# First loop of an LM tower kernel: masks moved to ScalarE, single factors, and the key and value tables made from two products each

## The reference, cut to what matters

```python
tok = wte[input_ids]                                   # rows of 192
Q = layer_norm(tok, gamma, beta) @ W_proj.T            # 8 heads of 64
V = tok @ W_val.T
Q_store = Q[:, :, :-2, :] * arrow_mask                 # tokens followed by a link id
Q_erase = Q_store / norm(Q_store)
erase = einsum('bhip,bhiq->hpq', Q_erase, einsum('bhip,hpq->bhiq', Q_erase, traces)) / denom
traces = 0.99 * (traces - erase) + 0.1 * einsum('bhip,bhiq->hpq', Q_store, V[:, :, 2:, :]) / denom
h = (Q shifted by one token @ traces) @ W_out.T
x = layernorm(h)
q, k, v = split(x @ W_qkv + b_qkv)                     # scores from q k^T
gw = softmax(gelu(v @ W_gp))
```

## Time and profile before

| what | value |
|---|---|
| median of three runs | 459.62 us |
| the profiled execution's own time | 457.82 us |
| its span on the core | 456.0 us |
| first loop, third to last product of queries | 18.48 to 60.65 us |
| between the loops, `prepare("kA")` to `mixed(0)` | 67.49 to 84.09 us |
| second loop | from 84.09 us on |
| TensorE's granted clock in these stretches | 1.00 |

### The profile page before, as it was taken

The page is one execution under the profiler, slowest core; times in us unless marked ns, Lnnn a source line. Parts: engine busy times, 40 slices in busy tenths (PEclk is TensorE's granted clock), DMA queues, the critical chain, the costliest instruction groups (busy, mean ns, idle before and its releaser), DMA issues.

```text
span 456.0 us, 8360 instructions
## 1 busy us (share of the span) xinstructions
PE 432.1 (95%) x3114; PEld 357.1 (78%) x3114; DVE 297.5 (65%) x779; ACT 228.1 (50%) x415; POOL 141.8 (31%) x235
## 2 busy tenths in 40 slices
PE   7898998998999999989999999999999899999995
PEld 5666666798788887878888888899975587787895
DVE  6799882486766657767777668766875253453564
ACT  5566742598833644744322557888864312122220
POOL 5666700375100007620003491013631331211310
PEclk9999999999999999999999999999999999999999
DMA  2115300200100000500000000004539999999404
GB/s 89 43 46 161 115 2 0 105 1 2 30 0 1 0 1 0 201 9 1 0 0 1 2 0 1 1 1 183 234 130 418 379 354 381 388 367 378 169 19 138
DMA packets 14231, 49.64 MB, mean 109 GB/s; under 512 B 3504, under 2 KB 8528, under 8 KB 9968
## 3 DMA queue, kind: packets, MB, share of 16 engines
q1 hardware_dynamic: 7584, 43.21, 25.3%
q0 software_dynamic: 2912, 3.37, 2.6%
q10 hardware_dynamic: 3696, 2.54, 1.8%
HBM read 45.94 MB, written 3.15 MB: 108 GB/s over the span
## 4 chain that ended last, share of the span: by engine, by line
PE 64%; DVE 13%; DMA 12%; POOL 4%; ACT 3%; issue 3%; SPq 0%; ACTq 0%; POOLq 0%; DVEq 0%
DMA w1r<-in_p_w 11%; PE ps L924 8%; PE ps L970 8%; PE ps L1126 5%; PE ps L1067 3%; PE ps L904 2%; PE ps L1096 2%; PE ps L950 2%; PE ps L951 2%; PE ps L952 2%; PE ps L954 2%; PE ps L953 2%; PE ps L1113 2%; DVE qw L1601 2%; DVE ss L1591 1%
## 5 line engine op out<-in xcount | busy, mean ns | idle before, releaser
L924 PE MATMUL ps<-pr,et 128*128 128x192 f32 x256 | 46.2, 331 | 1.6 <-DVE et L1790 1.2
L1126 PE MATMUL ps<-ys,ct 128*128 128x192 f32 x256 | 45.2, 330 | 0.7 <-DMA ys<-ys_dram 0.7
L1965 DVE TENSOR_TENSOR res<-ps,res 128x384 f32<-128x384 f32 x64 | 35.7, 558 | 14.2 <-PE ps L1126 9.7
L924 PEld LDWEIGHTS ps<-pr,et 128*128 128x128 f32 x256 | 41.2, 189 | 4.5 <-ACT et L1349 2.7
L1126 PEld LDWEIGHTS ps<-ys,ct 128*128 128x128 f32 x256 | 41.2, 190 | 4.1 <-issue 2.7
L590 POOL DMA_DIRECT2D ys<-ys_dram x32 | 19.7, 619 | 69.2 <-DMA ys_dram<-ysb 68.0
L1465 ACT ACTIVATE hs<-ps 128x384 f32<-128x384 f32 x16 | 7.8, 490 | 57.9 <-PE ps L1067 57.9
L506 POOL TENSOR_SCALAR ve<-mv 128x1 f32<-128x1 f32 x32 | 10.1, 314 | 81.7 <-DVE mv L1805 41.4
L1338 ACT ACTIVATE scs<-ps,pr 128x1024 f32<-128x1024 f32 x16 | 17.8, 1114 | 29.9 <-PE ps L872 29.9
L1956 DVE COPY ysb<-ps 128x192 f32<-128x192 f32 x16 | 5.7, 357 | 39.5 <-PE ps L1096 39.5
L1342 ACT ACTIVATE zz<-zz,nmx 128x1024 f32<-128x1024 f32 x16 | 18.4, 1151 | 26.0 <-DVE nmx L1784 25.8
(11 more groups left out here) (315 smaller groups left out, 1189.5 us busy)
## 6 DMA issues: line engine op xcount, KB each, us to landing
w1r<-in_p_w SPq DMA_DIRECT2D x16, 1152.0 KB, 19.4
w2r<-in_p_w SPq DMA_DIRECT2D x16, 1152.0 KB, 19.3
ys_dram<-ysb ACTq DMA_DIRECT2D x16, 96.0 KB, 8.7
ys<-ys_dram POOLq DMA_DIRECT2D x32, 48.0 KB, 7.2
phT<-in_p_phi SPq DMA_DIRECT2D x1, 1024.0 KB, 4.7
wT<-in_p_qkv SPq DMA_DIRECT2D x1, 774.0 KB, 5.8
out<-res SPq DMA_DIRECT2D x3, 192.0 KB, 3.4
out<-res ACTq DMA_DIRECT2D x3, 192.0 KB, 3.8
```

The lines of the kernel that those rows point to most:

```text
L924: last = mm(d[:, 0:D], et[:, k, :], pr[:, b * KT + k, 1:1 + D], start=(k == 0), stop=(k == KT - 1))
L1126: last = mm(bank(5 + q % 3)[:, h * D:(h + 1) * D], ct[:, u % 2, k + h, :], ys[:, t % YR, b, :], start=True, stop=True)
L1965: v.tensor_tensor(res[:, i:i + 2, :], bank(5 + q % 3)[:, 0:2 * D].rearrange("p (h d) -> p h d", h=2), res[:, i:i + 2, :], ALU.add).then_in ...
```

## The change

- `xm` is made for all 16 tiles by ScalarE (`masked` there), at the end of its step.
- The token table is passed with the last 64 columns of each row once more (`p_wte`, rows of 256 instead of 192 elements), `tok` has 256 columns, and `normalise` is one operation over 256 columns.
- `nmean` goes; GpSimd makes `nmr` from mean, `rstd` and -1. All factors are single. VectorE takes statistics two tiles ahead from step 3 on. GpSimd's gathers are re-ordered to this.
- `k`, `n` and `v` have two products each (A and B). For B, ScalarE copies the 66 rows to `B2`, then copies rows 0 to 63 of `B2` to `B1` (from SBUF); VectorE writes the remainder into rows 64 to 127 of `B1`.
- `kA` moves from in front of the update to behind the `n` products, its rounding to step 1 of the second loop; `mixed(3)`, which uses its bank, waits for that. `kB` stands where kB1 stood. The bias products go to bank 7 on their own, with their own copy by VectorE. `vB2` and its place in step 3 go.

```diff
-        tok = sb("tok", [P, NX, D], where=front0)
+        tok = sb("tok", [P, NX, XC], where=front0)
...
-        SETUP = ["beta", "kA", "kB1", "kB2", "nB2", "nB1", "nA", "vA", "vB1", "vB2"]
-        SETUP_BANK = [7, 7, 6, 7, 6, 4, 5, 5, 6, 5]
+        SETUP = ["beta", "kB", "nA", "nB", "kA", "vA", "vB"]
+        SETUP_BANK = [7, 6, 5, 4, 7, 6, 5]
...
-                    tok[:, g, :], None, a["L0_tok_wte"], bass.IndirectOffsetOnAxis(ap=ints[:, g:g + 1], axis=0)
+                    tok[:, g, :], None, a["p_wte"], bass.IndirectOffsetOnAxis(ap=ints[:, g:g + 1], axis=0)
...
+            def front_factors(i):
+
+                pool.wait_ge(m["front_stats"], i + 1)
+                link(nc.gpsimd.tensor_tensor(rstd[:, i:i + 1], ve[:, i:i + 1], mhalf[:, 0:1], ALU.pow))
+                nc.gpsimd.tensor_scalar(nmr[:, i:i + 1], mv[:, i, 0:1], rstd[:, i:i + 1], -1.0,
+                                        ALU.mult, ALU.mult).then_inc(m["front_rstd"], 1)
...
-            pool.wait_ge(m["xm_ready"], MV)
-            for i in range(MV, NT):
-                if i + 5 < NX:
-                    gather(i + 5)
-                masked(i)
-                if i % 2 == 0 and i + 2 < NT:
-                    front_factors(i + 2, i + 4)
+            for i in range(3, NT):
+                if i + 2 < KT:
+                    gather(i + 2)
+                elif i == KT - 2:
+                    gather(KT)
+                    gather(KT + 1)
+                elif i < KT + 2:
+                    gather(i + 3)
+                elif i == KT + 2:
+                    gather(KT + 5)
+                    gather(KT + 6)
+                elif i + 4 < NX:
+                    gather(i + 4)
+                front_factors(i)
...
-            prepare("kA", 1)
-
...
-            prepare("kB1", 0)
+            prepare("kB", 0)
...
-            pe.wait_ge(m["setup_taken"], at["kA"] + 1)
+            pe.wait_ge(m["setup_taken"], at["beta"] + 1)
             for t in range(HP):
-                mm(setup_bank("kB2")[:, 272 + 2 * t:274 + 2 * t], wpT[DB:DB + 1, 1, t * P:(t + 1) * P],
-                   ones[DB:DB + 1, 0:2], start=True, stop=True)
-            prepare("kB2", at["kA"] + 1)
-
-            pe.wait_ge(m["mm_ready"], 2)
-            pe.wait_ge(m["setup_taken"], at["kB2"] + 1)
-            for name, free in (("nB2", at["kB1"] + 1), ("nB1", 0), ("nA", 0)):
+                last = mm(bank(7)[:, 2 * t:2 * t + 2], wpT[DB:DB + 1, 1, t * P:(t + 1) * P], ones[DB:DB + 1, 0:2],
+                          start=True, stop=True)
+            last.then_inc(m["mix_done"], 1)
+
+            pe.wait_ge(m["mm_ready"], 3)
+            for name in ("nA", "nB"):
...
-            pe.wait_ge(m["setup_taken"], at["nA"] + 1)
+            prepare("kA", 0)
+            pe.wait_ge(m["setup_taken"], at["nB"] + 1)
+            pe.wait_ge(m["setup_hi"], hi_at["nB+"] + 1)
...
+                if i == 3:
+                    pe.wait_ge(m["setup_taken"], at["kA"] + 1)
...
-                if s == 3:
-                    prepare("vB2", at["vA"] + 1)
...
-                sc.activation(xh[:, i % 3, 0:D], tok[:, t, :], ACT.Identity, bias=nmr[:, i:i + 1], scale=rstd[:, i:i + 1])
-                sc.activation(xh[:, i % 3, D:D + DB], tok[:, t, P:D], ACT.Identity, bias=nmr[:, i:i + 1],
-                              scale=rstd[:, i:i + 1]).then_inc(m["xh_ready"], 1)
+                sc.activation(xh[:, i % 3, :], tok[:, t, :], ACT.Identity, bias=nmr[:, i:i + 1], scale=rstd[:, i:i + 1]
+                              ).then_inc(m["xh_ready"], 1)
+
+            def masked(i):
+                act.wait_ge(m["xh_ready"], i + 1)
+                sc.activation(xm[:, i, 0:D], xh[:, i % 3, 0:D], ACT.Copy, scale=mask[:, i:i + 1]).then_inc(m["xm_ready"], 1)
...
+                    sc.activation(B2, d[0:DB + 2, 0:n], ACT.Copy, scale=scale[1]).then_inc(m["setup_hi"], 1)
+                    act.wait_ge(m["setup_hi"], hi_at[name] + 1)
+                    sc.copy(B1[0:DB], B2[0:DB].bitcast(F32)).then_inc(m["setup_hi"], 1)
...
+                if 2 <= s <= NT:
+                    masked(s - 2)
+                if s == NT:
+                    masked(NT - 1)
...
-                if s in (1, 2, 4):
-                    round_v({1: "vA", 2: "vB1", 4: "vB2"}[s])
+                if s == 1:
+                    round_k("kA")
+                if s in (2, 3):
+                    round_v({2: "vA", 3: "vB"}[s])
...
+                    v.scalar_tensor_tensor(B1[DB:P], d[0:DB, 0:n], scale[1], f(B2[0:DB]), ALU.mult, ALU.subtract)
                     last = remainder(B2[DB:DB + 1, :], d[DB:DB + 1, 0:n], scale[2], B2[DB:DB + 1, :])
...
-                v.tensor_scalar(nmean[:, i:i + 1], mv[:, i, 0:1], -1.0, None, ALU.mult)
...
-                if s <= KT + 1:
-                    return {KT + 1: [KT + 2, KT + 3]}.get(s, [s + 1] if s >= 2 else [])
+                if s <= 3:
+                    return {2: [3], 3: [4, 5]}.get(s, [])
                 return [s + 2] if s + 2 < NT else []
...
-            for name in SETUP[4:7]:
+            dve.wait_ge(m["mix_done"], 3)
+            v.tensor_copy(wpn[:, :, XC:PC], bank(7)[:, 0:2 * HP].rearrange("p (t c) -> p t c", c=2)).then_inc(m["mm_ready"], 1)
+            for name in ("nA", "nB"):
                 round_n(name)
```

More of the change, by code:

```diff
@@ L44, in build @@
 def build(nc, a, out):
-    D = a["L0_tok_wte"].shape[1]
+    D = out.shape[-1]
     _, _, HD = a["p_wp"].shape
@@ L62, in build @@
     PC = P + 2 * DB + 2
-    CB1, CB2 = P, P + DB
+    CB2 = P + DB
     XC = P + 2 * DB
@@ L175, in build @@
         xm = sb("xm", [P, NT, D + 1], where=front)
-        nmean = sb("nmean", [P, NT], where=front)
         ss = sb("ss", [P, NT, HEADS], where=front)
@@ L364, in pass_tiles @@
             return []
-        SETUP = ["beta", "kA", "kB1", "kB2", "nB2", "nB1", "nA", "vA", "vB1", "vB2"]
-        SETUP_BANK = [7, 7, 6, 7, 6, 4, 5, 5, 6, 5]
+        SETUP = ["beta", "kB", "nA", "nB", "kA", "vA", "vB"]
+        SETUP_BANK = [7, 6, 5, 4, 7, 6, 5]
         at = {n: k for k, n in enumerate(SETUP)}
-        PARTS = {"A": (0, P), "B1": (CB1, P), "B2": (CB2, DB + 2)}
+        PARTS = {"A": (0, P), "B": (CB2, DB + 2)}
+        HI = [n + part for n in SETUP for part in (("", "+") if n[1] == "B" else ("",))]
+        hi_at = {n: k for k, n in enumerate(HI)}
         def setup_bank(name):
@@ L480, in _ @@
             for g in range(3):
                 gather(g)
-            front_factors(0, 1)
-            front_factors(1, 2)
+            for i in range(2):
+                front_factors(i)
             gather(3)
-            front_factors(2, 3)
+            front_factors(2)
             gather(4)
[L487 to L493, removed]
@@ L1250, in _ @@
             last.then_inc(m["update_taken"], 1)
-            round_k("kB1")
+            round_k("kB")
             act.wait_ge(m["mix_done"], 1)
@@ L1255, in _ @@
             last.then_inc(m["mm_ready"], 1)
-            round_k("kB2")
-            for name in SETUP[4:7]:
+            for name in ("nA", "nB"):
                 round_n(name)
@@ L1521, in round_off @@
             def round_off(name, scale, Ah, Al, B1, B2, n):
-                dve.wait_ge(m["setup_hi"], at[name] + 1)
+                dve.wait_ge(m["setup_hi"], hi_at[name] + 1)
                 d = setup_bank(name)
-                part = name[1:]
-                if part == "A":
+                if name[1:] == "A":
                     last = remainder(Al, d[:, 0:n], scale[0], Ah)
-                elif part == "B1":
-                    last = remainder(B1[DB:P, :], d[DB:P, 0:n], scale[1], B1[DB:P, :])
                 else:
+                    v.scalar_tensor_tensor(B1[DB:P], d[0:DB, 0:n], scale[1], f(B2[0:DB]), ALU.mult, ALU.subtract)
                     last = remainder(B2[DB:DB + 1, :], d[DB:DB + 1, 0:n], scale[2], B2[DB:DB + 1, :])
-                if name == "kB2":
-                    last = v.tensor_copy(wpn[:, :, XC:PC], d[:, 272:272 + 2 * HP].rearrange("p (t c) -> p t c", c=2))
                 last.then_inc(m["setup_taken"], 1)
@@ L1632, in _ @@
                 if s == 2:
-                    masked(0)
                     count()
-                if 2 <= s <= MV:
-                    masked(s - 1)
                 if s == KT + 2:
```

55 lines of the change are left out of this document (18 added, 37 removed).

## The result

The kernel after takes 452.92 us in the median of four runs (452.15 to 453.34), beside 459.84 us for the kernel before in its four; the ratio, with its 95% interval, is 0.9875 [0.9836, 0.9914] (of the two medians alone it would be 0.985). It was run twice more, beside other runs of before: 451.18 us (ratio 0.9817 [0.9778, 0.9855]) and 453.25 us (0.9895 [0.9878, 0.9912]). So it is faster by 1.1 to 1.8%, 5.2 to 7.9 us between medians; 9.05 us were forecast. Its profiled execution took 452.15 us, the shortest of its four, with a span of 450.3 us, against 457.82 and 456.0; that of the third repeat (451.58 us) is even 1.5 us shorter than the next one of its kernel, and no trace shows what the longer ones lose.

The account below looks back on a forecast made before the run. The first loop was taken as bound by a ring of statistics, factors, normalising, transposing and rounding, the stretch between the loops by TensorE's chain. Savings of 4.35, 4.3 and 0.4 us made 9.05: median 459.62 to 450.6 us, range 448 to 454.

Parts of the forecast that it names:

- First loop, the pace: First loop: steps fall from 3.24 to 2.85 us, TensorE and VectorE level; q_proj(15) at 56.3 instead of 60.65, saving 4.35 us.
- First loop, ScalarE's room: First loop: ScalarE's work per tile sums to 2.64 us, below 2.85; the cast some 0.4 us later has room.
- The tail of the first loop: From q_proj(15) to the first product of the update: carried over unchanged at 6.84 us.
- Start to q_proj(2): Ramp before the first loop: 0.1 us later for the mask on ScalarE, q_proj(2) at 18.58.
- Between the loops: Stretch between the loops: 16.6 us become 12.3, saving 4.3 us; bounds 3.3 and 4.7.
- Second loop: Second loop: `vB2` goes with 1.15 us, but only 0.4 us is kept as saving; bounds -0.4 and 1.1.
- Behind the second loop: Rest of the kernel behind the loops: no transfer tied to an absolute time, so the savings are carried through.
- The gather of 1024-byte rows: GpSimd's gathers in the first loop: longer rows slow them; at three times the gather, 469.5 us; chance 0.03.
- The port: First loop: a gather holds VectorE's clamp in nearly every tile; 2.7 us back, 453.3 us; chance 0.10.
- rival 3: Between the loops: `kA` is not covered, 1.26 us return, 451.9 us; chance 0.10.
- rival 2: First loop: ScalarE's masks come late, the cast waits, the step stays at 3.24 us; 454.9 us; chance 0.08.
- The sum: Whole kernel: 9.05 us saved; profiled execution from 457.82 to 448.8 us, median from 459.62 to 450.6 us.

Follow-up runs that it names:

- the third buffer: Also edit 6: the kernel after with three instead of two buffers for the masked queries `qm`, orders unchanged; 449.86 us, ratio 0.9789.
- experiment 1: The kernel after with ScalarE's mask `xm` moved from behind `qm` to in front of the squares; 450.88 us, ratio 0.984.
- Edits 2: The kernel after with VectorE's copy of the beta row and `eyeP` two steps earlier; 451.14 us, ratio 0.9827.
- experiment 8: The kernel after with mask ahead of the squares, beta row copied two steps earlier, and GpSimd's memset of `X1L` behind `cc`; 449.97 us, ratio 0.979.
- experiment 11: The kernel after with all sixteen masks on GpSimd instead of ScalarE; 457.77 us, ratio 0.9986.
- experiment 3: The kernel before with only the table part (two products per table, `kA` behind the `n` products, bias products in their own bank); 453.39 us, ratio 0.9875.
- experiment 7: The kernel after with `kA` and its rounding ahead of the `n` products; 452.14 us, ratio 0.9837.
- experiment 4: The kernel before with only the first loop's part (masks on ScalarE, single factors, doubled columns), tables as before; 457.56 us, ratio 0.9984.

## Why the prediction was right or wrong

**First loop, the pace: right.** TensorE's floor of 2.85 us is the pace. In the execution without the long step q_proj(2) to q_proj(15) takes 37.65 us, in the third buffer's 37.61; the prediction's terms give 37.7. The twelve steps take 34.33 us (forecast 34.4, with 0.2 for the wrap, of which one step of 2.91 shows 0.06), the last 3.32 (3.29). ScalarE's and GpSimd's prices fit.

**First loop, ScalarE's room: wrong, and this is the step that failed.** The prediction put it so: "The mask comes last in ScalarE's step; behind it waits the cast of the next tile. By these rows that cast is then some 0.4 us later after its q_proj than now, but a step has more room than this". It compared sums of durations with the step and looked behind the mask, but not in front of it. There stands `qm`, which waits for gram products of two tiles before; in the kernel before it waited once up to 60 us, for 0.9 us (2.2 up to the loop's end). Now it waits in nearly every tile, 7.8 us with the mask and the cast behind. In the ten even steps a step indeed has the room. It has none where `qm` is let go late near the start: 1.2 us in two of three executions, and experiment 1, with the mask ahead of the wait, cuts this to 0.2. Nor has it any at the end of the loop, where the cast behind `qm` and two masks holds the last `XL` for 0.95 us.

**The tail of the first loop: a missing term.** q_proj(15) to bs was carried over as it stood. It had no slack: TensorE already waited 0.21 us for `cc` in the kernel before, and it hangs on VectorE, not on TensorE. The late cast took 0.66 us of VectorE's lead, the failed step again, and the clamp beside a memset another 0.35; both came up as a wait: 1.0 us in all three executions. Edits 2, 6 and 8 each take it away (6.69, 6.87, 6.68).

**Start to q_proj(2): mis-sized.** 0.1 us was taken, 0.34 to 0.52 measured. In the ten profiles with the new loop (experiment 11 left out) q_proj(2) starts between 18.72 and 19.30, in the two with the old loop at 18.48 and 17.88: some of it is spread between executions, but all ten are later. The prediction had the landing of the gathers "covered as now". At the start it is not: up to 60 us VectorE's statistics wait for gathered rows twice, 1.9 us in all, in both profiles with the old loop, and four times, 3.3 to 4.0 us, in all ten with the new one, each time ahead of q_proj(2). Whether the longer rows, the statistics' new order or that of the gathers makes this was not tried.

**Between the loops: right.** Forecast 4.3 (12.3 us), measured 4.2 in each execution and in experiment 3. The terms: `kA` 1.26 as taken; the part up to the bias columns 0.1 (taken: nothing); from there to the tables 2.06 (2.03); tables and tail 0.80 (1.02), since 73.63 to 77.88 is 4.25 us and not 4.03: the two products take 2.71 as priced, the tail 1.54 instead of 1.31. These products and the tail read now

```profile
73.63 2.87 PE L749 MATMUL ps<-mm,wpn 128*128 128x192 f32 x16 [0.26 <-DVE wpn L1646]
76.34 0.60 PE L615 MATMUL ps<-wT 128*128 128x257 f32 x2
76.86 0.70 PE L616 MATMUL ps<-wT 64*128 64x257 f32 x2
77.88 0.35 PE L596 MATMUL ps<-nAh,XH 128*128 128x192 f32 x1 [0.32 <-DVE nB L1518]
```

```profile
76.99 0.41 DVE L1527 SCALAR_TENSOR_TENSOR nB<-ps,cols,nB 64x192 fp32r<-64x192 f32 x1 [0.88 <-ACT nB L1199]
77.41 0.41 DVE L1518 SCALAR_TENSOR_TENSOR nB<-ps,cols,nB 1x192 fp32r<-1x192 f32 x1
```

`kA` (76.34 to 77.56) ends ahead of the last remainder of `nB` (to 77.82), so it is covered, by a quarter of a microsecond. Experiment 7 gives its price where it isn't, 1.25 for the 1.26 taken.

**Second loop: mis-sized.** 0.4 us forecast, 0.04 to 0.10 measured. `vB2` goes with its 1.15 us, but the factors come later against TensorE. The waits of ScalarE for `nmr` in the first 21 us of the loop, first of the kernel before, then of the kernel after:

```profile
ACT x1t L1300 <- POOL nmr L512: 0.8, 2, 0.5
```

```profile
ACT x1t L1299 <- POOL nmr L506: 2.6, 5, 0.9
```

The prediction named this ("the pace soon hangs on statistics and factors") and took too little for it. It comes with the tables: these waits are 2.6 us in experiment 3 and 0.8 in experiment 4. VectorE's remainders for `kA` and `vA` don't cause it, since VectorE waits for TensorE behind each, and in experiment 7, where `kA`'s isn't there, the waits are 2.6 us too. Behind the two for `vB` the fourth statistics start without a wait:

```profile
80.49 0.37 DVE L1691 BATCH_NORM_STATS2 st<-ps 128x6 f32<-128x192 f32 x1 [0.54 <-PE ps L600]
...
82.18 0.37 DVE L1691 BATCH_NORM_STATS2 st<-ps 128x6 f32<-128x192 f32 x1 [0.55 <-PE ps L600]
...
83.91 0.37 DVE L1691 BATCH_NORM_STATS2 st<-ps 128x6 f32<-128x192 f32 x1
```

They start 6.03 us behind mixed(0), against 5.25 in the kernel before. That `vB`'s remainders cause the rest fits, and was not tried.

**Behind the second loop: taken as carried through.** 0.05 to 0.65 us are lost there. The group of the last stage's products waits for stored tiles 0.7 us in the kernel before and 1.4 in the kernel after:

```profile
L1120 PE MATMUL ps<-ys,ct 128*128 128x192 f32 x256 | 45.2, 330 | 1.4 <-DMA ys<-ys_dram 1.4
```

It is 0.9 in both repeats, though the first repeat loses as much behind gs as the kernel after, so this wait is not the whole of it. The stretch varies between executions of one kernel, and nothing ties it to the change.

**The rivals.** The gather of 1024-byte rows falls (1.01 us). The port falls as priced: ten more meetings were feared; beside the gathers the clamp stays at 0.17 in all steady steps. But there it falls into the first 0.6 us of a gather. In the kernel before two clamps (0.44 at 41.87, 0.34 at 48.53), in experiment 3 two (0.44 and 0.33) and in experiment 11 two (0.67 at 29.62, 0.71 at 46.56) last until 0.1 to 0.15 us behind the end of a gather, with GpSimd's mask next. So the change got away from this by its phases and with the mask off GpSimd, which the prediction did not work out; no run separates the two. The port came true in one place that wasn't looked at, a memset:

```profile
L1588 DVE TENSOR_SCALAR ss<-ss x15: 171/172/525, 19.4 to 61.4; 128x8 f32<-128x8 f32 x15
```

The Trainium skill (SBUF — State Buffer, SBUF: two separate sides) has VectorE and GpSimd share a pair of ports with an exclusive lock; the clamps agree: the one beside the memset ends 0.03 to 0.04 us behind the memset's end in the kernel before (0.27 us), the kernel after (0.53) and with the third buffer (0.53), and the long clamp of experiment 8 (0.47) moved with the memset. `kA` uncovered (rival 3) falls for this order. The kept ring (rival 2) falls as a pace, but its reason, "ScalarE's masks come late, the cast waits", is what happened at the two ends of the loop.

**The sum.** The profiled execution took 452.15 us and not 448.8. The 3.35 us are 0.24 at the start, 1.1 of the long step, 1.0 of the tail, 0.1 between the loops, 0.3 in the second loop and 0.6 behind it. The median of 452.92 us stands at the upper end of the range (448 to 454), which was drawn for the port and for `kA`. Neither cost what was feared, so that it comes so near is luck and speaks for nothing in the sum.

**What stays open:** why `qm(2)` is let go over 1 us late in four of these six profiles and in experiment 1. Only ScalarE waits for this signal at that time, so no second engine tells whether the signal or ScalarE was late. The rival of experiment 1, ScalarE's supply of instructions, is not excluded, and the traces do not speak for it: one transfer on the instruction queue q8 lies between 21.5 and 23.5 us in all ten profiles with the masks on ScalarE, with the late `qm(2)` and without it.

## What to carry to other kernels

When an operation moves to an engine with room, do not compare sums with the step alone: look at what stands in front of it in that engine's order, and which wait it will be queued behind. A wait that cost nothing while nothing was behind it becomes a cost of the moved work; one more buffer (here 1.3 us, more than the 0.9 us that the loop's part gained in its own run) takes it away again, and the moved work ahead of the waiting instruction takes part of it. And the serial tail behind a loop must be followed on the engine that sets its end: TensorE already waited 0.2 us for VectorE there, so what delayed VectorE's last operations showed in full.

## What the runs showed of the hardware

- A gather of 128 rows takes GpSimd 1.01 us with rows of 1024 bytes and 1.02 with 768.
- A VectorE clamp of 128x8 elements in SBUF takes 0.17 us alone and in the first 0.6 us of a gather, 0.33 to 0.71 in six cases late in a gather that a mask on GpSimd followed, and 0.27 to 0.53 beside GpSimd's memset of 64x1024, where it ends 0.03 to 0.04 us behind the memset. It is held until the other operation is done, so its price depends on when it starts.
- One ScalarE operation over 256 columns with bias and scale from columns takes 0.61 us, against 0.55 and 0.43 for 192 and 64; on ScalarE the next operation starts about 0.1 us ahead of the end of the one before (`qm` at 54.45 takes 0.69, the masks start at 55.04), so a sum of durations is above its pace. On GpSimd it was below it in experiment 11: 2.67 us of durations, 2.93 from gather to gather.
- The same program can lose 1.2 us in one step or not, from one execution to the next, with the clock at 1.00 (the kernel after and its first repeat).
